# Fused attention and two mixtures of experts: norms and router of the live tiles in one pass, the output product inside the next tile's first block of keys

## The reference

```python
# attention: 16 heads of 64, one null key, one key and value head for all
xn = layernorm(x, g_in); q = xn @ Wq * scale; k, v = split(xn @ Wkv)
sim = q @ k.T + bias;  sim = where(causal_mask | masked_key, neg, sim)
y = layernorm(softmax(sim) @ v @ Wo, g_out)
# router of the first mixture (16 experts, each takes its 128 best tokens)
t = y / rms(y) * norm_w;  logits = t @ rw.T + rb
x = x + experts(t, top tokens per expert, gates)
x = x + second_mixture(shared_and_gated(x))
```

## Time and profile before

| | |
|---|---|
| median of three runs | 925.21 us (918.31, 926.66, 925.21) |
| profiled execution | 919.85 us, span 918.1 us |
| busy, share of the span | PE 692.0 us (75%), DVE 484.8 (53%), POOL 356.0 (39%), ACT 287.8 (31%) |
| attention block | 36.1 to 196.9 us of the span |
| selection of tokens | 196.9 to about 253 |
| `bias_sb<-in_bias` | 4 transfers of 1024 KB, 12.8 us to landing |
| `w_sb<-in_w` | 32 transfers of 1024 KB, 8.4 us to landing |
| `table<-row` | 4 rows of a tile each, 128.0 KB, 3.1 us to landing |

### The profile page before, as it was taken

The page is one execution under the profiler, slowest core; times in us unless marked ns, Lnnn a source line. Parts: engine busy times, 40 slices in busy tenths (PEclk is TensorE's granted clock), DMA queues, the critical chain, the costliest instruction groups (busy, mean ns, idle before and its releaser), DMA issues. The chain is left out here.

```text
span 918.1 us, 14493 instructions
## 1 busy us (share of the span) xinstructions
PE 692.0 (75%) x4394; PEld 628.4 (68%) x4395; DVE 484.8 (53%) x1127; ACT 287.8 (31%) x643; POOL 356.0 (39%) x466
## 2 busy tenths in 40 slices
PE   1466677620579999659899999945489889999990
PEld 1356667510478989527788888724489889999990
DVE  3354545458611111156877777748267557766640
ACT  1214424410023233124233333233235424544320
POOL 2122021000034445412344443223385567676672
PEclk9666675565679999969999999976799999999995
DMA  8372092030039998249401000020363352222234
GB/s 260 78 161 46 21 296 106 0 112 4 0 103 312 304 298 247 36 143 353 155 19 35 17 17 0 14 79 0 118 140 95 61 137 37 43 43 46 44 45 112
DMA packets 78386, 94.98 MB, mean 103 GB/s; under 512 B 8480, under 2 KB 69344, under 8 KB 78176
## 3 DMA queue, kind: packets, MB, share of 16 engines
q1 hardware_dynamic: 64160, 76.80, 27.0%
q0 software_dynamic: 11536, 14.94, 9.8%
q10 hardware_dynamic: 2640, 2.62, 0.9%
HBM read 77.68 MB, written 18.56 MB: 105 GB/s over the span
## 5 line engine op out<-in xcount | busy, mean ns | idle before, releaser
L1320 PE MATMUL f_pt<-xparts,cparts 128*128 128x512 f32 x480 | 119.2, 398 | 0.0
L1857 ACT ACTIVATE nh<-npH,c_sb 128x288 f32<-128x288 f32 x128 | 64.1, 501 | 121.0 <-PE npH L1829 121.0
L1320 PEld LDWEIGHTS f_pt<-xparts,cparts 128*128 128x128 f32 x480 | 88.7, 191 | 18.5
L1775 POOL DMA_INDIRECT acc<-nyg,si x51 | 91.3, 1790 | 13.9 <-issue 13.6
L108 POOL TENSOR_TENSOR held<-ones 128x1 f32<-128x1 f32 x134 | 48.5, 362 | 109.4 <-DVE nyg L1876 53.2
L1308 POOL TENSOR_TENSOR hidl<-sums,hidh 128x512 fp32r<-128x512 f32 x40 | 52.1, 1302 | 93.3 <-ACT hidh L1362 93.3
L1827 PE MATMUL npH<-nxh,w1l 128*128 128x288 f32 x256 | 77.9, 304 | 1.6 <-DVE nxl L1869 1.6
L1838 PE MATMUL npY<-nhh,w2l 128*128 128x288 f32 x256 | 78.3, 306 | 0.0
L1840 PE MATMUL npY<-nhh,w2h 128*128 128x288 f32 x256 | 76.7, 300 | 0.0
L1839 PE MATMUL npY<-nhl,w2h 128*128 128x288 f32 x256 | 76.6, 299 | 0.0
L1829 PE MATMUL npH<-nxh,w1h 128*128 128x288 f32 x256 | 76.3, 298 | 0.0
(11 more groups left out here) (345 smaller groups left out, 1510.7 us busy)
## 6 DMA issues: line engine op xcount, KB each, us to landing
w_sb<-in_w SPq DMA_DIRECT2D x32, 1024.0 KB, 8.4
w_sb<-in_v SPq DMA_DIRECT2D x16, 1024.0 KB, 10.5
bias_sb<-in_bias SPq DMA_DIRECT2D x4, 1024.0 KB, 12.8
acc<-zrow SPq DMA_DIRECT2D x1, 2056.0 KB, 16.4
sums<-acc SPq DMA_DIRECT2D x4, 514.0 KB, 5.3
x_sb<-in_x SPq DMA_DIRECT2D x1, 2048.0 KB, 9.9
table<-row ACTq DMA_DIRECT2D x1, 2048.0 KB, 14.6
b_sb<-in_b SPq DMA_DIRECT2D x1, 2048.0 KB, 8.2
```

The source lines that it names most:

```text
L1320: ins = pe.matmul(pp[:, c % 2], cparts[:, u, wn, at], xparts[:, xn, k, chunk], start=(k == 0 and (wn, xn) == (0, 1)), stop=(k == KD - 1 an ...
L1775: pool.indirect_dma_start(acc1, bass.IndirectOffsetOnAxis(ap=si3[:, s:s + 1], axis=0), yg[:, s], None, compute_op=ALU.add).then_inc(scatte ...
```

## The change

The tile's heads are turned and multiplied with `wo_sb` not behind its last block but inside the next tile's first block of keys (`first`), which gets its own copy of the block's code; the dead tiles' output goes the same way in the first tile. The product goes to `pS`, is kept by VectorE in `Y`, and its statistics in `st_all`. `Y` lies in the space of experts 1 to 3's weights, so SP loads only expert 0 beside the attention, and the others when all rows have been written. Norms and router of the live tiles come after the last output product: moments of all tiles at once (`all_moments`), a loop over the tiles that centres and scales, the moments again, and a loop (`post`) with the row, the router and the table's write for each tile. `norms(0)` for the dead tiles stays.

```diff
@@ -238,6 +238,26 @@
...
+        def query_tiles(eng, name, on_tile, on_keys, after):
...
+                    with eng.Fori(first, QT) as qt:
+                        on_tile(b, qt, eng.snap(nq), eng.snap(nk))
+                        on_keys(b, qt, first, eng.snap(nq), eng.snap(nk), True)
+                        eng.reg_add(nk, nk, 1)
+                        with eng.If(first < qt):
+                            with eng.Fori(first + 1, qt + 1) as kt:
+                                on_keys(b, qt, kt, eng.snap(nq), eng.snap(nk), False)
...
+            Y = w1_sb[:, 1:RING].rearrange("p u k f -> p (u k f)")[:, 0:T * D].rearrange("p (t d) -> p t d", d=D)
...
+                    tiles = sp.snap(live_tiles(sp, "sp_att", None, keys))
+                    load_expert(sp, w1, w2, 0, 0)
+                    sp.wait_ge(y_stat, tiles + 2)
+                    sp.wait_ge(row_out, done(16 * tiles + 16))
+                    for u in range(1, RING):
                         load_expert(sp, w1, w2, u, u)
...
+                    def keep_row(b, qt, n):
+                        mine = Y[:, ds((n + 1) % T, 1)].rearrange("p a d -> p (a d)")
+                        pool.wait_ge(row_ready, n + 1)
+                        pool.tensor_copy(mine, row[:]).then_inc(row_kept, 1)
+                    live_tiles(pool, "pool_post", keep_row)
...
+                    def project(half):
+                        for c in range(FC // 2 * half, FC // 2 * (half + 1)):
+                            ins = pe.matmul(pS[:, 0, 0:D], OT[:, c], wo_sb[:, c], start=(c == 0), stop=(c == FC - 1))
+                        if half:
+                            ins.then_inc(o_proj, 1)
...
+                    def queries(b, qt, nq, nk):
+                        pe.wait_ge(pt_ready, done(nk * 4))
...
+                        pe.wait_ge(k_done, done(nk * 2))
...
-                        logits(nq + 1)
...
+                        pe.wait_ge(y_kept, done(nq) if first else done(nq + 1))
...
+                        if first:
+                            turn_heads(nq)
...
+                            if first and g == 0:
+                                pe.wait_ge(ot_ready, nq + 1)
+                            if first and g == 1:
+                                pe.wait_ge(ot_high, nq + 1)
...
                             weigh(g - 1)
+                            if first and g <= 2:
+                                project(g - 1)
                         weigh(3)
...
-                    logits(pe.snap(tiles) + 1)
...
+                    pe.wait_ge(y_kept, done(tiles))
+                    turn_heads(tiles)
...
+                    project(0)
+                    project(1)
+
+                    def post(b, qt, n):
+                        pe.wait_ge(row_ready, n + 1)
+                        logits(n + 1)
+                    live_tiles(pe, "pe_post", post)
 
...
+                    def heads_high(n):
+                        act.wait_ge(ot_done, n * 2 + 2)
+                        act.activation(OT[:, FC // 2:FC].rearrange("p c q -> p (c q)"), pT[:, 1], ACT.Copy).then_inc(ot_high, 1)
...
-                        columns(nq + 1)
-                        rows_out(nq + 1, table[ds(act.snap(last) * P, P), 0:D], row[:])
-
...
                         exps(0)
+                        if first:
+                            heads_high(nq)
                         for g in range(1, 4):
                             exps(g)
                             keep(g - 1)
                         act.activation(st[:, ALPHA], st[:, DIF], ACT.Exp).then_inc(alpha_ready, 1)
                         keep(3)
...
+                    for m in range(2):
+                        act.wait_ge(n_step, m * NSTEP + 9)
+                        act.activation(mv_all[:, 6], mv_all[:, 5], ACT.Sqrt).then_inc(n_root, 1)
...
+                    def post(b, qt, n):
+                        columns(n + 1)
+                        act.wait_ge(row_kept, done(n + 1))
+                        act.dma_start(table[ds(b * N + qt * P, P), 0:D],
+                                      Y[:, ds((n + 1) % T, 1)].rearrange("p a d -> p (a d)")).then_inc(row_out, 16)
+                    live_tiles(act, "act_post", post)
+                    act.wait_ge(row_out, done(16 * tiles + 16))
...
+                    def router(n, keep):
+
+                        dve.wait_ge(lg_done, n + 1)
+                        dve.tensor_tensor(lgr[:], pT[:, 1, 0:E0], rb_b[:], ALU.add).then_inc(lg_row, 1)
+                        dve.wait_ge(lg_row, n + 1)
+                        dve.wait_ge(lt_done, n + 1)
+                        keep()
...
+                    dve.tensor_copy(O[:], repeat(nv[:], H)).then_inc(o_ready, 1)
+                    dve.memset(st_all[:], 1.0).then_inc(y_stat, 1)
...
-                        dve.tensor_copy(O[:], repeat(nv[:], H)).then_inc(q_step, 1)
...
+                    def keep_output(n):
+                        mine = Y[:, ds(n % T, 1)].rearrange("p a d -> p (a d)")
+                        of_mine = st_all[:, ds(n % T, 1)].rearrange("p a s -> p (a s)")
+                        dve.wait_ge(y_stat, n + 1)
+                        dve.wait_ge(o_proj, n + 2)
+                        dve.tensor_copy(mine, pS[:, 0, 0:D]).then_inc(y_kept, 1)
+                        dve.wait_ge(y_kept, done(n + 1))
+                        dve.bn_stats(of_mine, mine).then_inc(y_stat, 1)
...
+                        if first:
+                            turned(nq)
                         add(3)
...
+                        if first:
+                            keep_output(nq)
                         dve.wait_ge(alpha_ready, nk + 1)
-                        put(18, dve.tensor_tensor(O[:], O[:], bcast(st[:, ALPHA], DH), ALU.mult))
+                        put(18, dve.tensor_tensor(O[:], repeat(nv[:], H) if first else O[:], bcast(st[:, ALPHA], DH), ALU.mult))
...
-                        turned(nq + 1)
...
-                    norms(tiles + 1, tiles + 1, keep)
+
+                    tiles = dve.snap(query_tiles(dve, "dve_att", queries, keys, after))
+                    turned(tiles)
+                    keep_output(tiles)
+                    dve.wait_ge(y_stat, tiles + 2)
...
+                    def all_moments(squares):
+
+                        first, second = st_all[:, :, 1], st_all[:, :, 4]
+                        link(dve.tensor_tensor(mv_all[:, 1], first, second, ALU.add))
+                        link(dve.tensor_tensor(mv_all[:, 2], first, second, ALU.subtract))
+                        link(dve.tensor_tensor(mv_all[:, 4], st_all[:, :, 2], st_all[:, :, 5], ALU.add))
+                        link(dve.tensor_scalar(mv_all[:, 0], mv_all[:, 1], 0.5, None, ALU.mult))
+                        link(dve.tensor_tensor(mv_all[:, 3], mv_all[:, 2], mv_all[:, 2], ALU.mult))
+                        link(dve.tensor_scalar(mv_all[:, 5], mv_all[:, 4], 1.0 / D, EPS, ALU.mult, ALU.add))
+                        link(dve.tensor_tensor(mv_all[:, 4], mv_all[:, 0], mv_all[:, 0], ALU.mult))
+                        link(dve.scalar_tensor_tensor(mv_all[:, 5], mv_all[:, 3], 0.25, mv_all[:, 5], ALU.mult, ALU.add))
+                        if squares:
+                            link(dve.tensor_tensor(mv_all[:, 5], mv_all[:, 5], mv_all[:, 4], ALU.add))
+                        else:
+                            link(dve.tensor_copy(mv_all[:, 1], mv_all[:, 0]))
+                        dve.wait_ge(n_root, 2 if squares else 1)
+                        link(dve.reciprocal(mv_all[:, 7], mv_all[:, 6]))
+
+                    all_moments(False)
+
+                    def centred(b, qt, n):
+                        mine = Y[:, ds((n + 1) % T, 1)].rearrange("p a d -> p (a d)")
+                        dve.tensor_scalar(mine, mine, mv_all[:, 0, ds((n + 1) % T, 1)], mv_all[:, 7, ds((n + 1) % T, 1)],
+                                          ALU.subtract, ALU.mult).then_inc(b_step, 1)
+                        dve.wait_ge(b_step, done(n * 3 + 1))
+                        dve.tensor_tensor(mine, mine, go_b[:], ALU.mult).then_inc(b_step, 1)
+                        dve.wait_ge(b_step, done(n * 3 + 2))
+                        dve.bn_stats(st_all[:, ds((n + 1) % T, 1)].rearrange("p a s -> p (a s)"), mine).then_inc(b_step, 1)
+                    live_tiles(dve, "dve_centred", centred)
+                    dve.wait_ge(b_step, done(tiles * 3))
+                    all_moments(True)
+
...
+                        tile = b * QT + qt
+
+                        def keep():
+                            dve.tensor_scalar(lg_all[:, ds(tile, 1)].rearrange("p a e -> p (a e)"), lgr[:], 1.0, None,
+                                              ALU.mult).then_inc(lt_kept, 1)
+                            dve.tensor_scalar(LT_all[:, ds(tile * P, P)], pT[0:E0, 0, 0:P], 1.0, None,
+                                              ALU.mult).then_inc(q_done, 1)
+
+                        dve.wait_ge(row_turned, n + 1)
+                        dve.wait_ge(row_out, done(16))
```

(35 more changed lines are left out.)

90 lines of the change are left out of this document (41 added, 49 removed).

## The result

The changed kernel takes **938.37 us** (median of six runs, 932.69 to 943.04) against 925.93 for the kernel before beside it (six runs, 918.31 to 939.32): the ratio is **1.0173, 95% interval 1.0135 to 1.0210**. A second timing (e5) gave 1.0122 (1.0067 to 1.0176). Ratios leave out executions in a slower state, so they are not quotients of the medians given beside them. The change makes the kernel between one and two per cent slower. The profiled execution took 938.97 us with a span of 937.3; its mean granted clock is 0.852, before it was 0.855.

The account below looks back on a forecast made before the run. Bound: TensorE's full later part of key blocks and 20.75 us serial transitions, which the change attacks. Attention -19.4, pass +21.5, SP's queue +16.0 sum to +18.1, 938 us on the profiled scale; forecast 940, between that and the runs' scale, range 925 to 953.

Parts of the forecast that it names:

- First tile: Start of attention: the first tile's scores start at 59.35 instead of 64.69, -5.35 us.
- Two transitions: From one tile's last weighing to the next tile's scores: 7.0 us in place of 20.75, -13.75 each, -27.5 together.
- a give-back of 11.8 at 5.66: Tile transitions: with the query product at the lower clock (5.66 us), a transition would give back 11.8 us.
- Three first blocks: Each tile's first key block takes in turning, two copies and the output product: 4.5 us a block, +13.5.
- the prediction's upper bound: First key blocks: +6.5 us if all ran at the lower clock (product 5.82) and nothing was given back.
- Pass: After the last tile's statistics: late norms and router passes take 30.5 us in place of 9.0, +21.5.
- SP's queue: End of the block: six late expert loads hold up the router's columns, so selection waits, +16.0 us.
- Rival, upper clock throughout: TensorE keeps the upper clock through the attention: -22 us against the forecast, 916 us in all; chance 0.07.
- the rival of free columns: Router's columns not held up by the late loads: sum +2, 922 to 928 us; chance 0.10.
- the last block's 0.50: Last key block: dense 10 us at granted clock 0.50, taken as evidence against the upper-clock rival.

Follow-up runs that it names:

- e5: The changed kernel again, unchanged, timed beside the kernel before: 934.72 us against 924.14, ratio 1.0122.
- e3: The changed kernel with the router's columns fetched on ScalarE's queue instead of SP's, the six late loads left in place: 927.07 us, ratio 1.0112 to the kernel before.
- e1: The changed kernel with the six late expert loads issued in the next block, behind the selection's small transfers: 914.85 us against 921.17 before, ratio 0.9925.
- e8: e6 plus four unread 128x256 products per block, in TensorE's gap between scores and first turning: 905.30 us against 924.14 for the kernel before, ratio 0.9768.
- e6: e1 with the first live tile's turning and product of the dead tiles' output skipped: 916.65 us, ratio 0.9910 to the kernel before.
- e10: The kernel before with only the four unread 128x256 products per block added between scores and first turning: 923.30 us against 924.73, ratio 0.9990.
- e9: e7 and e8 together, late norms between tiles plus four unread products per block: 906.59 us against 924.73 for the kernel before, ratio 0.9822.
- e7: e6 with each tile's norms put back between tiles, one tile late, and no norms pass over all tiles: 908.75 us, ratio 0.9856 to the kernel before.

## Why the prediction was right

The forecast was 940.0 (925 to 953), slower with 0.76; the sum on the profiled execution's scale was 938, and the profiled execution after took 938.97. Each step is at its place; single terms are off by up to 3.7 us and cancel. That the sum came within 1 us is luck; that every step took place as described, but for the inner working of SP's queue, is not.

- *First tile*: -4.0 us for -5.35. The query product starts at 50.58, not 49.0, and takes 6.39 in place of 5.66; the null product behind it gives 0.85 back. The late start fits loops' heads that I left out (TensorE idle 4.54 with no releaser).
- *Two transitions*: -10.8 and -13.8 for -13.75 each. The second is the forecast's 7.0 to the hundredth (6.99). The first has 1.4 of idle time at the loops' heads and 1.6 of lower clock more. The prediction had priced the second (a give-back of 11.8 at 5.66) and not the first.
- *Three first blocks*: 20.8, 20.3 and 18.6 us, against 16.6, 16.6 and 16.7: +9.8 for +13.5. The size of the product was right: its two halves take 5.68, 5.68 and 4.78 us together, for 5.23. Too small was what I let the block get back: with the 0.6 of ScalarE's copy it is 2.1, 2.6 and 3.4 us, for 1.3. In blocks two and three the scores take 2.06 us (before 3.79), and the weighing between the halves takes 1.0 to 1.4 (before 1.81): the upper clock reached more than the last weighing, for which alone I had taken 0.8 off. A half takes 3.73 at the lower level, so the whole would be 7.5 there; the 5.82 that the prediction's upper bound took for the lower level was itself a mix, and that bound was too low. The fourth block gave 0.8 more. With the transitions this makes -19.4 at the last weighing, where -19.4 stood: the two mis-sized terms cancelled.
- *Pass*: +19.4 for +21.5. A router pass is 4.14 us (182.15 to 186.29), not 4.66; moments are 2.5 each, and loop heads 1.5 to 1.6 and 1.3 to 1.6 in place of 2.0 and 1.34.
- *SP's queue*: +17.6 (last row in the table to selection, 21.6 for 4.0) for +16.0. Size right, working half right. I let bytes alone set the time, and SP's issuing "fall inside" them. e3 shows that the issuing holds the block for some 7 us and that being on SP's queue is under a third of the price. The sum comes out alike because the columns then wait only for what the loads have left: SP issues while the loads already run. The Trainium skill's rule (DMA: Bandwidth & Descriptors, "Queues, rings and completion order"), that a small transfer starts behind what stands in its ring, agrees with the changed kernel against e3 (13.3 and 8.4 us to landing). By that rule alone e3 should have landed them after about 3.2, as e1 did.
- *Rival, upper clock throughout*: it did not happen, but part of it did. From 60 to 156 us the clock is 0.77, before it was 0.67, and three of four blocks read their scores sooner. Its price of 22 us was never tested whole; e8, at 0.81, took 7.3 us off e6's attention.

For the rival of free columns (922 to 928), e1 is the test: without the hold-up the kernel is 0.75% faster than before, at 915 beside 921. The sum said +2.1; the profiled execution has its selection 4.9 us earlier than before. The 7.0 between them are 3.4 of an attention shorter than the changed kernel's (e5), 1.5 of first scores that start earlier than there, and 2.1 of the over-priced pass.

The clock is where the prediction's reasoning was weakest. It took the last block's 0.50 as a sign that dense work does not raise the clock. Rows of e6 and e8 show more: the clock right behind the gap goes with what TensorE did in it, 3.12 us idle (0.50 from 66.7 to 73) or filled with products (0.96). It does not explain all: from 73 to 78 both are at 0.50. The Trainium skill (TensorE: Matmul & The Clock Gate, "What's actually happening") says that the gate sets the clock by how busy the engine has recently been; e8 and e10 agree (0.70 to 0.81, 0.67 to 0.81), and so does e9 against e7 (0.72 to 0.80); e10 and e9 without a gain that shows in the ratios.

## What to carry to other kernels

Space that is freed late makes loads late: before work is gathered behind a stage, ask whose buffers it keeps, and issue the small transfer that someone waits for ahead of the loads that become possible at that moment. Moving a product from a serial stretch into the next tile's block paid (12 us). Batching short chains into a late pass did not (8 us won, 19.4 paid), because its loops and routers have nothing beside them. A gain on TensorE counts only if no other engine stands between its end and the next step.

## What the runs showed of the hardware

- **Spare work can buy time.** Sixteen products that nobody reads, four in each block, made one kernel faster by 1.4% (ratio 0.9910 to 0.9768, e6 to e8), and another not measurably (0.9990, e10). Skipping a useless product bought nothing measurable (0.9925 and 0.9910, e1 and e6).
- **GpSimd delays VectorE.** A VectorE product of two tensors took 1.22 us when it started before GpSimd's 512-wide addition (82.44 and 82.53 before) and 2.34 when it started with it (81.33 in e10). One-element operations on two tensors took up to 1.23 instead of 0.15 beside it (e9), an operation with one tensor and a constant 0.15 (107.67 in e9). The Trainium skill (GPSIMD Engine Reference, "Specifications") says that GpSimd's ways into the on-chip memory are shared with VectorE where an instruction has two inputs there; these rows agree.
- **Issuing can take long.** In the changed kernel SP's first four loads of 1024 KB took 0.4 to 1.0 us to issue, the fifth 4.28, the sixth 0.93 and the transfer behind them 4.33; in e1 one load took 6.47. It looks as if SP waits for room in its queue; no run tests that. An engine that only issues can so hold up a block's end.
